# A last sample's rank product in the rounded format, low parts in another order, and its sums on another engine

## The reference, cut to what matters

```python
def xcond(x_cls, x, noise, ...):            # B=4 samples, 1024 rows each, D=512
    k = ln(x) @ wk + bk; v = ln(x) @ wv + bv
    slots = q_mu + exp(q_logsig) * noise
    for _ in range(3):
        prev = slots
        q = ln(slots) @ wq + bq
        attn = softmax(q k^T / scale over the slots) + 1e-8
        attn = attn / sum over the rows n
        slots = (attn^T v) @ wu + bu + prev
        slots = gelu(ln(slots) @ w1 + b1) @ w2 + b2 + slots
        slots = ln(slots + x_cls)
    return slots
def ffn(x):                                 # the routed part
    idx = top_k(x @ w_router, 256)          # per sample
    x_sel = x[idx]; h = rmsnorm(x_sel)
    x_attn = causal attention of h, 16 heads of 32, then W_out
    h2 = rmsnorm(x_sel + x_attn)
    return x with x_sel + x_attn + (silu(h2 W1) * (h2 W2)) W3 in the rows idx
x = x + xcond(cond, ctx, layernorm(x))
x = x + ffn(layernorm(x))
```

## Time and profile before

| | |
|---|---|
| executions | 2356.34, 2357.03, 2360.32 us |
| the profiled execution | 2363.11 us, its span 2361.4 us |
| TensorE busy | 2312.7 us, 98% of the span |
| VectorE, ScalarE, GpSimd busy | 1605.5, 975.1, 993.7 us |
| mean granted clock of TensorE | 0.990 |

### The profile page before, as it was taken

One profiled execution on the slowest core, in us unless ns is written; L12 is line 12 of the kernel. 1 busy time (PEld: TensorE's weight loads), 2 busy tenths in 40 slices (PEclk: granted clock), 3 DMA queues, 4 the chain that ended last, 5 costly groups with the idle time before them and its releaser, 6 DMA issues.

```text
span 2361.4 us, 30933 instructions
## 1 busy us (share of the span) xinstructions
PE 2312.7 (98%) x11557; PEld 1900.6 (80%) x11557; DVE 1605.5 (68%) x2915; ACT 975.1 (41%) x1646; POOL 993.7 (42%) x1345
## 2 busy tenths in 40 slices
PE   8999999999999999999999999999999998999998
PEld 4888888888878888887888888888888887777886
DVE  7777657757477575768757567785775769965542
ACT  2566443343333333333333433334333345756432
POOL 1576235151453515435354452544535157733200
PEclk9999999999999999999999999999999999989999
DMA  5587000000052000013400001350000012204330
GB/s 201 198 312 252 1 1 1 1 1 19 32 193 75 1 23 5 14 50 138 139 6 19 9 10 54 115 162 5 10 19 1 19 55 80 91 10 131 106 112 18
DMA packets 87125, 158.58 MB, mean 67 GB/s; under 512 B 10801, under 2 KB 33337, under 8 KB 83134
## 3 DMA queue, kind: packets, MB, share of 16 engines
q1 hardware_dynamic: 82838, 150.26, 18.5%
q0 software_dynamic: 2688, 6.31, 0.9%
q10 hardware_dynamic: 1450, 0.04, 0.0%
HBM read 106.21 MB, written 50.37 MB: 66 GB/s over the span
## 4 chain that ended last, share of the span: by engine, by line
PE 79%; DVE 12%; POOL 4%; ACT 2%; issue 2%; DMA 0%; ACTq 0%; DVEq 0%; POOLq 0%
PE ps L221 24%; PE ps L223 24%; PE ps L222 24%; PE ps L1501 3%; DVE moments L2002 3%; POOL gT1l L2621 2%; DVE slots L2401 2%; DVE tbuf L2395 1%; DVE zTl L2043 1%; DVE tbuf L2388 1%; PE ps L1657 1%; DVE mx L2348 1%; ACT prob L1905 1%; PE ps L447 1%; PE ps L1486 1%
## 5 line engine op out<-in xcount | busy, mean ns | idle before, releaser
L221 PE MATMUL ps<-zTh,kTl 128*128 128x512 f32 (+1 forms) x912 | 334.1, 366 | 10.6 <-DVE zTl L2043 8.0
L223 PE MATMUL ps<-zTh,kTh 128*128 128x512 f32 (+1 forms) x912 | 326.3, 358 | 0.0
L222 PE MATMUL ps<-zTl,kTh 128*128 128x512 f32 (+1 forms) x912 | 326.2, 358 | 0.0
L221 PE MATMUL ps<-vh,prob_lo 128*128 128x512 f32 x768 | 306.1, 399 | 0.0
L223 PE MATMUL ps<-vh,prob_hi 128*128 128x512 f32 x768 | 300.1, 391 | 0.0
L222 PE MATMUL ps<-vl,prob_hi 128*128 128x512 f32 x768 | 299.3, 390 | 0.0
L2043 DVE TENSOR_TENSOR zTl<-ps,zTh 128x512 fp32r<-128x512 f32 x224 | 151.2, 684 | 200.4 <-ACT zTh L1770 200.4
L2519 POOL TENSOR_SCALAR rs_m<-mv_m 128x1 f32<-128x1 f32 x96 | 55.3, 576 | 544.4 <-DVE mv_m L2004 542.7
L1905 ACT ACTIVATE prob<-ps,nb 128x1024 f32<-128x1024 f32 x96 | 107.2, 1117 | 256.5 <-DVE nb L2353 256.0
L221 PEld LDWEIGHTS ps<-zTh,kTl 128*128 128x128 f32 x912 | 173.0, 190 | 44.1 <-DVE zTl L2043 15.7
L1752 ACT ACTIVATE zbuf<-slots,rs_m 128x512 f32<-128x512 f32 x96 | 78.4, 816 | 303.4 <-POOL rs_m L2524 303.4
(11 more groups left out here) (331 smaller groups left out, 5744.1 us busy)
## 6 DMA issues: line engine op xcount, KB each, us to landing
ctx<-in_ctx_dram SPq DMA_DIRECT2D x8, 1024.0 KB, 7.5
slots<-in_x_dram SPq DMA_DIRECT2D x8, 1024.0 KB, 6.7
kT_d<-kTh SPq DMA_DIRECT2D x6, 1024.0 KB, 7.7
kT_d<-kTl SPq DMA_DIRECT2D x6, 1024.0 KB, 9.6
s_d<-slots SPq DMA_DIRECT2D x6, 1024.0 KB, 5.1
v_d<-vh SPq DMA_DIRECT2D x6, 1024.0 KB, 9.6
v_d<-vl SPq DMA_DIRECT2D x6, 1024.0 KB, 11.6
kTh<-kT_d SPq DMA_DIRECT2D x3, 2048.0 KB, 10.6
```

The source lines that it names most:

```text
L221: nc.tensor.matmul(out, ll, rh, start=start, stop=False)
L222: nc.tensor.matmul(out, lh, rl, start=False, stop=False)
L223: return nc.tensor.matmul(out, lh, rh, start=False, stop=stop)
```

## The change

1. **The rank product.** The blocks `place` and a copy of the token numbers (`tokr`, each number in two columns) are in the rounded format (float32r), and `I` multiplies each block with two columns. `place_tokens` has one small copy more. `chosen_tokens` reads every second column.
2. **Low parts at a sample's end.** VectorE does `z_lo` 2 and 3 and `z_stats` 5 to 7 in another order among `residual`, `gained` and `new_slots`; in the last round `h_lo(0, 0)` and `h_lo(0, 1)` stand ahead of `residual(4)`.
3. **The last sample's sums.** `x + slots` of the last sample is done by GpSimd (`last_x1`): tiles 0 and 1 ahead of `row_scale(1)`, 2 and 3 ahead of the loop, 4 to 7 in iterations 1 and 2. VectorE keeps the moments; those of tiles 1 and 2 go into iterations 0 and 1. `final(0)` stands behind `gather(2)`. The sums for the output go from iterations 2 to 7 into iterations 8 to 15, one in each, and SP sends the sums x + slots and the scores before them.
4. **Around the gather.** The squares for the norm of sample 0 go from VectorE to ScalarE (`row_squares`, iteration 14). `gather(3)` stands ahead of `normalise`, `gathered_stats(3)` ahead of `again_lo(0)`, and `norm_gathered(3)` and `norm_rows(3)` ahead of `keep(19)`.

```diff
-    place = [at("place0", [P, 4, CAP], 164 * KB), at("place1", [P, 4, CAP], OR + 6 * KB)]
+    place = [at("place0", [P, 4, CAP], 164 * KB, f32r), at("place1", [P, 4, CAP], OR + 6 * KB, f32r)]
     places = at("places", [P, CAP], 185 * KB)
+    tokr = small("tokr", [P, NT, 2], f32r)
     g1c = small("g1c", [P, C])
...
             bank_free(("I", B - 1, 0))
-            pe.wait_ge(sem("counted"), (B - 1) * (3 * NT + 2) + 3 * NT + 1 + NT)
+            pe.wait_ge(sem("counted"), (B - 1) * (3 * NT + 2) + 3 * NT + 1 + NT + 1)
             out = bank(UNIT_BANK["I", B - 1, 0])
...
                 for j in range(NT):
-                    last = nc.tensor.matmul(out[:, t:t + 1], place[j // 4][:, j % 4, cut(t)], tokf[:, j:j + 1],
+                    last = nc.tensor.matmul(out[:, cut(t, 2)], place[j // 4][:, j % 4, cut(t)], tokr[:, j, :],
                                             start=(j == 0), stop=(j == NT - 1))
...
+        def row_squares(q):
+            for t in range(QT):
+                act.wait_ge(sem("y_ready"), q * QT + t + 1)
+                if t:
+                    act.wait_ge(sem("ssf_ready"), q * QT + t)
+                A.activation(sqj[:, :], yrow(q * QT + t), ACT.Square, accum_out=ssq[:, 4 + t:5 + t])\
+                    .then_inc(sem("ssf_ready"), 1)
         def final_norm(j):
...
                 exps(n + 3)
+            if q == 2 and i == 3:
+                norm_gathered(3)
+                act.wait_ge(sem("tr_h2"), QT)
+                norm_rows(3)
             if q == 3 and i == 2:
...
                 h_hi(q + 1, 1)
-            if q == 2 and i == 3:
-                norm_gathered(3)
-                act.wait_ge(sem("tr_h2"), QT)
-                norm_rows(3)
             if n + 3 < PAIRS and not rows_out:
...
                     qk_out(2, 2 * i - 4)
+                if i == 6:
+                    row_squares(0)
                 if i == 7:
...
         invert(1)
-        final_stats(B - 1, 1)
-        final_stats(B - 1, 2)
         def place_tokens():
...
             dve.wait_ge(sem("counted"), n)
+            V.tensor_copy(tokr[:, :, :], tokf[:, :].rearrange("p (k o) -> p k o", o=1).to_broadcast([P, NT, 2]))\
+                .then_inc(sem("counted"), 1)
             for j in range(NT):
...
             dve.wait_ge(sem("colsum_done"), B * ROUNDS + 2)
-            V.tensor_scalar(tokg[:, cut(B - 1, QT)], bank(UNIT_BANK["I", B - 1, 0])[:, 0:QT], float((B - 1) * S), None,
-                            ALU.add).then_inc(sem("idx_ready"), 2)
+            V.tensor_scalar(tokg[:, cut(B - 1, QT)],
+                            bank(UNIT_BANK["I", B - 1, 0])[:, 0:2 * QT].rearrange("p (t o) -> p t o", o=2)[:, :, 0],
+                            float((B - 1) * S), None, ALU.add).then_inc(sem("idx_ready"), 2)
...
             if q == 0:
+                if i == 0:
+                    final_stats(B - 1, 1)
                 if i == 1:
-                    final_stats(B - 1, 3)
+                    final_stats(B - 1, 2); final_stats(B - 1, 3)
                 if i == 2:
...
                 if i == 7:
-                    squares(0)
                     place_tokens()
...
                         dve.wait_ge(sem(f"x1_out{k}"), B * 16)
+                    gathered_stats(3)
                     again_lo(0)
                     add_row(1, 0)
-                    gathered_stats(3)
                 if i == 3:
...
-    def routed_pool(pool, rstd_two, gather, row_scale, row_rms, base, scatter):
+    def routed_pool(pool, rstd_two, gather, row_scale, row_rms, last_x1, base, scatter):
         G = nc.gpsimd
...
+        last_x1(0, 1)
         row_scale(1); row_rms(1)
...
         scatter(B - 2, range(5, NT))
+        last_x1(2, 3)
         for n in range(PAIRS):
             q, i = divmod(n, HP)
+            if (q, i) == (2, 1):
+                pool.wait_ge(sem("idx_ready"), B * 2)
+                for k in range(2):
+                    pool.wait_ge(sem(f"x1_out{k}"), B * 16)
+                pool.nop(nofuse=True)
+                gather(3)
             if n + 2 < PAIRS:
...
                 if i == 0:
-                    final(0)
                     pool.wait_ge(sem("tok_in0"), 2 * 16)
                     gather(2)
+                    final(0)
                 if i == 1:
+                    last_x1(4, 5)
                     final(1)
                 if i == 2:
-                    base(B - 1, 0)
+                    last_x1(6, 7)
                 if i == 3:
...
                     row_scale(2); row_rms(2)
-                if i == 4:
-                    base(B - 1, 1); base(B - 1, 2)
                 if i == 5:
                     final(3)
-                    base(B - 1, 3); base(B - 1, 4)
-                if i == 6:
-                    base(B - 1, 5)
+            if q == 1:
                 if i == 7:
-                    base(B - 1, 6); base(B - 1, 7)
-            if q == 1:
+                    rms(0)
+                base(B - 1, i)
                 if i == 2:
...
                            allow_small_or_imprecise_dtypes=True).then_inc(sem("pool_step"), 1)
-                if i == 7:
-                    rms(0)
             if q == 2:
-                if i == 1:
-                    pool.wait_ge(sem("idx_ready"), B * 2)
-                    for k in range(2):
-                        pool.wait_ge(sem(f"x1_out{k}"), B * 16)
-                    pool.nop(nofuse=True)
-                    gather(3)
                 if i == 2:
...
             tokens_in(sp, B - 2, "tok_in0")
+            for k in range(2):
+                sp.wait_ge(sem("x1_ready"), b * NT + 4 * k + 4)
+                sp.dma_start(four(x1_d[b * S + k * 512:b * S + (k + 1) * 512, :]), stg_l[:, cut(k, 4), :])\
+                    .then_inc(sem(f"x1_out{k}"), 16)
+            scores_out(b)
+            sp.dma_start(last_row[:, :], score_d[b].partition_broadcast(P)).then_inc(sem("score_in"), 16)
             for j in range(NT):
-                if j == NT - 2:
-                    scores_out(b)
-                    sp.dma_start(last_row[:, :], score_d[b].partition_broadcast(P)).then_inc(sem("score_in"), 16)
                 sp.wait_ge(sem("base_ready"), b * NT + j + 1)
                 sp.dma_start(a["out"][b, cut(j), :], lastb[:, j % 2, :]).then_inc(sem(f"base_out{j % 2}"), 16)
-                if j % 4 == 3:
-                    k = j // 4
-                    sp.dma_start(four(x1_d[b * S + k * 512:b * S + (k + 1) * 512, :]), stg_l[:, cut(k, 4), :])\
-                        .then_inc(sem(f"x1_out{k}"), 16)
             routed_sp(sp)
...
             def final_stats(b, j):
-                dve.wait_ge(sem(f"x_in{j // 4}"), (HS // 2 + b + 1) * 16)
-                V.tensor_tensor(stg_l[:, j, :], stg_l[:, j, :], slots[:, j, :], ALU.add).then_inc(sem("x1_ready"), 1)
                 dve.wait_ge(sem("x1_ready"), b * NT + j + 1)
...
                     queries_lo(3)
+                    h_lo(0, 0); h_lo(0, 1)
                     residual(4); gained(4)
                     residual(5); new_slots(4); gained(5)
-                    h_lo(0, 0); h_lo(0, 1)
                     residual(6); new_slots(5); gained(6)
...
                     residual(3); new_slots(2); gained(3)
+                    z_stats(4)
                     z_lo(yn, 0); z_lo(yn, 1)
+                    z_stats(5)
                     new_slots(3)
-                    z_stats(4)
-                    residual(4); gained(4)
-                    z_stats(5); z_stats(6)
-                    residual(5); new_slots(4); gained(5)
+                    residual(4)
+                    z_lo(yn, 2)
+                    gained(4)
+                    z_stats(6)
+                    residual(5)
                     z_stats(7)
-                    z_lo(yn, 2); z_lo(yn, 3)
+                    z_lo(yn, 3)
+                    new_slots(4); gained(5)
                     residual(6); new_slots(5); gained(6)
...
+            def last_x1(*tiles):
+                for j in tiles:
+                    pool.wait_ge(sem(f"x_in{j // 4}"), (HS // 2 + B) * 16)
+                    pool.wait_ge(sem("slots_ready"), ALL_TILES - NT + j + 1)
+                    G.tensor_tensor(stg_l[:, j, :], stg_l[:, j, :], slots[:, j, :], ALU.add).then_inc(sem("x1_ready"), 1)
             def base(b, j):
...
                 slot_round(g, g == B * ROUNDS - 1)
-            routed_pool(pool, rstd_two, gather, row_scale, row_rms, base, scatter)
+            routed_pool(pool, rstd_two, gather, row_scale, row_rms, last_x1, base, scatter)
```

## The result

The kernel after took 2354.76 us (median of 19 executions, 2351.78 to 2358.26), the kernel before, on the same chips, 2360.19 us (median of 19, 2356.04 to 2362.58): a ratio of 0.998, 95% interval 0.9973 to 0.9987. That is 5.4 us, where 12.5 were forecast, and the time lies above the range (2336 to 2353). The three executions of before that were known had a median 3.2 us under that of the 19, and the profiled one (2363.11 us) stood 2.9 us above it, not 6.1. The profiled execution of after took 2353.49 us, its span is 2351.8 us, its granted clock 0.993 where that of before was 0.990.

What follows compares the result with a forecast made beforehand. TensorE, busy 98% of the span, was taken as the bound, leaving gains in idle stretches, lower-clock stretches and the rank product. Terms -5.5 + 1.5 - 7.2 - 1.3 = -12.5 us; 2363.1 - 12.5 - 6.1 = 2344.5 us, range 2336 to 2353.

Steps and rivals of the forecast that it cites:

- Low parts at the samples' ends: Ends of samples 0 to 2: reordering shortens TensorE's waits and avoids lower clock, -5.5 us; bounds 1.7 and 12 us gain.
- The rank product: Rank product: sixteen matmuls in 1.8 us instead of 32 in 5.4, full clock behind, -7.2 us; bounds -2.5 and -8.
- 3.6 + 0.8 + 2.9: Rank product's gains: shorter matmuls 3.6 us, the wait before them 0.8, the stretch behind at full clock 2.9.
- The output sums: Iterations 8 to 15: eight 1.29 us sums fit where GpSimd waits for VectorE's reciprocals, costing nothing; uncovered, up to 10.3 us.
- the forecast's own form of that rule: Moved sums: each of eight 1.29 us GpSimd sums could hold VectorE up, 10.3 us; all reaching TensorE gives 2354.8 us.
- The last round and iterations 0 to 12: Last round and early attention: waits move to scores(0) and turn(3), GpSimd's queue runs late, +1.5 us; bounds +6 and -5.
- The gather: Gather and T(3, 0): gather starts some 9 us earlier, wait falls to 2.4 us, -1.3 us; bounds 0 and -6.3.
- the middle term: The term for the last round and iterations 0 to 12: a loss of 1.5 us, bounds +6 and -5.
- the queue eats it: Rival, chance 0.11: ends give 1.7 us, product 2.5, gather 0, attention loses 2.5; 2355.3 us.
- the 6.1 us taken off: Whole-kernel sum: the profiled execution, 2363.11 us, taken as 6.1 us above the median of 2357.03, subtracted at the end.

Runs made afterwards that it cites:

- b_ends: The kernel before with only the new order of low parts and moments at the ends of samples 0 to 2: 2357.70 us, ratio 0.999.
- b_self: The kernel before, unchanged, run again with the granted clock of every execution listed: 2360.21 us median of 12.
- b_product: The kernel before with only the rank product in the rounded format, copy of token numbers included: 2356.07 us, ratio 0.9986.
- b_product_ends: The kernel before with the rounded rank product and the new order at the samples' ends, nothing else: 2352.62 us, ratio 0.9968.
- after_self: The kernel after, unchanged, run again: 2355.99 us, ratio to before 0.9978.
- a_h_back: After with both kinds of sums back as before, and h_lo(0, 0) and h_lo(0, 1) behind residual(5) again: 2349.60 us.
- a_best: After with both kinds of sums back, plus low part 5 ahead of new_slots(7), gained(6) behind residual(7), token-number copy in iteration 8: 2346.27 us, ratio to before 0.9938.
- a_best2: a_best with ScalarE's pairs of final_norm an iteration later too: 2345.34 us, ratio to before 0.9938.

## Why the prediction was wrong, point by point

**Low parts at the samples' ends** (-5.5 us). In the profile it came out nearly to the row: waits of 0.76 and 1.42 us at sample 1 (forecast 0.9 and 1.5), 1.40 at sample 2, in all 6.2 us. In the time of the kernel it was 2.5 ± 0.6 us. The term's mechanism was right; its size was mostly clock, and was taken from one profile, whose window shows 0.50 over the whole 4 us behind the wait, where another profile of the same kernel had the lower level for part of it (0.64). From the wait to the first pair of logits that made 12.10 us in the first and 10.69 in the second. That the profile met the forecast was partly luck: fifteen profiles with the new order reach the last wait for `gT1l` of the last round anywhere between 1954.8 and 1959.3 us (mean 1956.7), three with the old one between 1959.5 and 1962.0 (mean 1961.0). By these the term is worth 4.3 us, by the times 2.5; its size is not known better than that.

**The rank product** (-7.2 us). Sixteen matmuls in 1.92 us came as forecast. Alone the part gave 3.9 us. The step that failed is the price of what it replaces and of what comes instead: 5.43 us and 7.0 us behind it, both clock-bound, were set against the full clock throughout. From `scores(19)` to `scores(21)` the float32 product took 17.3, 17.3 and 14.1 us (before, b_ends, b_self), the rounded one 10.9 and 12.4 (b_product, b_product_ends): the forecast took the dearest of the first and about 10.1 for the second. In the whole change it gave less still, 2.5 us in the first two profiles (17.3 to 14.8), and nothing against b_self's 14.1, because of the next point. (The terms named in the forecast, 3.6 + 0.8 + 2.9, make 7.3, not 7.2.)

**The output sums** (0). "Where GpSimd waits for VectorE's reciprocals several us in each iteration" was true, and the wrong cover to name. Their cost was not on GpSimd: the sum of iteration 15 held a comparison of VectorE for 1.0 us, just ahead of the product that TensorE waits for. Taken back, they are worth 1.7 ± 1.2 us. The forecast had the rule for it and put it aside because "the steps it meets are mostly reads of PSUM"; the eight comparisons read and write SBUF. The row agrees with the Trainium skill, SBUF — State Buffer, section Who interferes with whom, by which tensor_scalar can be an instruction that needs the ports it shares with GpSimd, and then stands for the whole of GpSimd's: 1.32 us of GpSimd, 1.36 us of VectorE. That the time worked out from the forecast's own form of that rule, 2354.8 us, is the measured one is luck: it stood for 10.3 us in which eight sums of GpSimd hold VectorE up, and the rows show 1.0 us of that ahead of the product. In which of its modes the comparison ran, no row shows.

**The last round and iterations 0 to 12** (+1.5 us, bounds -5 and +6). Here lies the error of mechanism, the step of the forecast that failed most. The wait moved from `Q(0, 0)` to `scores(0)`, 2.67 us as forecast (2.6), and h_lo was worth 2.2 ± 1.0 us. ScalarE's idle stretch and TensorE's 2.1 us at `turn(3)` (forecast about 3) are there too. What I left out is VectorE: I counted its eight sums as gone, and did not write down that the moments left behind it now wait for GpSimd, 5.7 us at tile 4 (4.7 in after_self), with the masked scores queued behind them. And I set the new waits against the old ones as if either could be had; with the sums on VectorE the old waits shrank by the rest of the change. The sums x + slots cost 5.4 us and h_lo gave 2.2: a loss of 3.2 where 1.5 was forecast, before the 1.7 of the output sums.

**The gather** (-1.3 us). The wait before `T(3, 0)` fell from 3.57 to 2.88 us (forecast 2.4). With the squares off VectorE, which I had booked under the product, the part is worth 3.5 us in after.

**The sum.** Ends and product together 7.0 (forecast 12.7), gather 2.7 (from b_product_ends, 2352.7, to a_h_back, 2350.0), h_lo 2.2, sums -7.1: 4.8 us, where means give 4.9 (2359.8 - 2354.9) and medians 5.4. Each step is the difference of two neighbouring kernels, so that they add up proves nothing; each has an error of 0.5 to 1.0 us. Of the shortfall of 7.6 us (12.5 against 4.9), 5.7 us are ends and product, with the clock priced from one execution; 3.4 us are the middle term (the sums' loss of 7.1 less h_lo's 2.2, against a loss of 1.5); and the gather gave 1.4 more than forecast. The rival that came nearest is *the queue eats it* (2355.3 us, 0.11). It named the right places, a loss in the attention and small ends and product; that its time fits so well is partly luck, since its loss was too small (2.5, measured 4.9) and so were its gains (4.2, measured 7.0 and 2.7). Its time also rests on the 6.1 us taken off, where 2.9 would have been right.

**Still open:** what decides, behind a wait or behind none, whether the lower level comes and for how long. No run here sets it, and it moves a single profile by more than most parts of this change are worth.

## What to carry to other kernels

A stretch at the lower clock in one profile is a chance, not a cost: before it goes into a sum, profile the same kernel again, or set the executions' times against their clocks. When you compare a stretch between profiles, begin it ahead of the waits that differ. When a step moves to another engine and its readers stay, write down for every reader what it now waits for and what is queued behind it; emptying the busy engine by 5 us of sums made it stand 5.7 us in one wait. And GpSimd's spare time is not free where VectorE then does SBUF work on the path.

## What the runs showed of the hardware

- Where a wait was followed by the lower level differed between executions of one kernel. After a wait of 2.6 us at the end of sample 1 the window of 4 us behind it shows 0.50 in one profile of before. The 4.5 us from just before TensorE goes on show 0.50 there too (1112.69 to 1117.19), and 0.64 in the next profile (1112.50 to 1117.00). Executions of before reached from a mean clock of 0.988 to 0.993, and from 2365 to 2357 us with it.
- From `scores(19)` to `scores(21)`, with the rounded product between, it took 13.2 to 14.8 us in the six profiles with a wait of 1.6 or 1.7 us before the product, 10.9 to 12.4 in the three with 0.6 or 0.8, 14.3 and 16.9 in the two with 1.2 and 2.4, and with none 9.8 in three and 11.3 in two (a_best, a_best2). Full clock behind the sixteen matmuls was seen in b_product (1.00) and not in b_product_ends (0.69), after the same wait of 0.84 us.
- A comparison of 0.34 us took 1.20 and 1.36 us beside a GpSimd instruction of two SBUF inputs, in float32 and in the rounded format alike; writing the rounded format cost nothing by itself (336 to 342 ns).
